# Moving the output gating of a head pair ahead of the next pair's scores in a fused LayerNorm, attention and int8 gate kernel

## The reference

```
xn = layernorm(x)                             # x: 4 x 4096 x 1024
q, k, v = split(xn @ qkv_weights)             # 16 heads of 64
a = softmax(causal(q @ k.T / 8))
s = a @ v
x_q = clip(round(xn / x_scale), -128, 127)    # x_scale = amax(|xn|) / 127, per row
g = silu((x_q @ weight_q.T) * x_scale * weight_scale + bias)
out = x + s * g
```

## Time and profile before

| | us |
|---|---|
| median of 3 runs | 1623.84 |
| lowest, highest | 1619.31, 1631.77 |
| the profiled execution's time | 1625.46 |
| its span, slowest core (core 4) | 1623.9 |
| spans of the eight cores | 1610.6 to 1623.9 |
| mean granted TensorE clock of the eight cores | 0.788 to 0.821 |

### The profile page before, as it was taken

How to read it: one execution, slowest core, us unless ns; L and a number is a source line. 1 busy time by engine, 2 the same in 40 slices (tenths; PEclk the granted TensorE clock), 3 DMA queues, 4 the chain that set the end, 5 groups by cost and what they waited for, 6 DMA issues and landing times.

```text
span 1623.9 us, 17793 instructions; the slowest of 8 cores (1610.6 to 1623.9 us)
## 1 busy us (share of the span) xinstructions
PE 1133.3 (70%) x5161; PEld 475.8 (29%) x5200; DVE 573.7 (35%) x1086; ACT 718.6 (44%) x905; POOL 301.3 (19%) x412
## 2 busy tenths in 40 slices
PE   0335545455565568887978887888688888888886
PEld 0112212212222225443333333333232333333332
DVE  0483472744735542137246227222621110110000
ACT  0121221212211123444354474466447787777776
POOL 1440421503324531013022012011200000000000
PEclk9867759567575666757977997888899998899998
DMA  7110000100002211011011011001000000000000
GB/s 114 52 40 0 26 27 0 39 14 26 26 13 65 64 47 40 26 52 53 7 46 46 7 52 40 7 21 40 20 7 20 14 14 14 14 21 11 9 14 20
DMA packets 24463, 47.46 MB, mean 29 GB/s; under 512 B 4272, under 2 KB 7472, under 8 KB 24368
## 3 DMA queue, kind: packets, MB, share of 16 engines
q1 hardware_dynamic: 15552, 25.34, 5.2%
q0 software_dynamic: 8816, 20.98, 5.2%
HBM read 40.54 MB, written 8.39 MB: 30 GB/s over the span
## 4 chain that ended last, share of the span: by engine, by line
PE 36%; DVE 23%; ACT 20%; issue 8%; POOL 5%; DMA 5%; DVEq 1%; ACTq 0%; POOLq 0%; SPq 0%
ACT eT L772 16%; PE Oa L789 5%; PE pm L551 4%; PE Ob L793 4%; PE pm L534 3%; DMA xst<-x 3%; DVE t_r L430 3%; PE sT L727 3%; DVE t_b L433 3%; PE pm L843 3%; PE pm L581 3%; PE pm L847 3%; DMA w8n<-w 2%; DVE t_g L428 2%; DVE bnst L240 2%
## 5 line engine op out<-in xcount | busy, mean ns | idle before, releaser
L772 ACT ACTIVATE eT<-sT 128x1024 bf16<-128x1024 f32 (+1 forms) x576 | 548.4, 952 | 331.1 <-PE sT L733 192.8
L789 PE MATMUL Oa<-eT,v_aug 128*65 128x512 bf16 (+1 forms) x576 | 245.3, 426 | 2.8 <-ACT eT L772 0.4
L793 PE MATMUL Ob<-eT,v_aug 128*65 128x512 bf16 (+1 forms) x576 | 233.2, 409 | 0.0
L727 PE MATMUL sT<-qT,kTa 64*128 64x512 bf16 x448 | 182.8, 417 | 63.0 <-ACT eT L772 61.5
L733 PE MATMUL sT<-qT,kTa 64*128 64x512 bf16 x448 | 185.7, 424 | 0.0
L892 POOL DMA_DIRECT2D out<-outs x32 | 24.4, 763 | 800.6 <-DVE outs L885 700.3
L828 DVE TENSOR_TENSOR wpr<-Oa,gT 64x512 bf16<-64x512 f32 x32 | 21.9, 683 | 370.0 <-PE Ob L793 369.2
L301 PE MATMUL sT<-Wqk,xnK 128*128 128x512 bf16 x244 | 106.5, 611 | 51.4 <-ACT xnK L289 40.3
L727 PEld LDWEIGHTS sT<-qT,kTa 64*128 64x128 bf16 x448 | 40.2, 94 | 267.0 <-issue 265.0
L789 PEld LDWEIGHTS Oa<-eT,v_aug 128*65 128x65 bf16 x576 | 68.7, 119 | 101.2 <-issue 88.8
L551 PE MATMUL pm<-Wv,xnq 128*128 128x512 bf16 x247 | 74.6, 452 | 27.9 <-DVE v_aug L558 21.8
(11 more groups left out here) (122 smaller groups left out, 1581.4 us busy)
## 6 DMA issues: line engine op xcount, KB each, us to landing
xst<-x SPq DMA_DIRECT2D x96, 256.0 KB, 2.9
xres<-xr POOLq DMA_DIRECT2D x32, 256.0 KB, 3.6
out<-outs POOLq DMA_DIRECT2D x32, 256.0 KB, 2.8
Wqk<-wq POOLq DMA_DIRECT2D x1, 1024.0 KB, 14.2
Wqk<-wk POOLq DMA_DIRECT2D x1, 1024.0 KB, 24.1
Wv<-wv POOLq DMA_DIRECT2D x1, 1024.0 KB, 30.4
w8n<-w POOLq DMA_DIRECT2D x4, 256.0 KB, 2.6
wscb<-wsc SPq DMA_DIRECT2D x4, 0.5 KB, 5.2
```

What stands on the lines that cost most here:

```text
L727: t.matmul(sT[par][:, o:o + w], kTa[0:64, P, 128 * jb:128 * jb + 128], qT[P][0:64, qb + o:qb + o + w], start=True, stop=True), waits=w0)
L772: s.activation(eT[pe3][:].rearrange("p (b n) -> p b n", b=2)[:, :, o:o + w], sT[par][:].rearrange("p (b n) -> p b n", b=2)[:, :, o:o + w], ...
L789: sc.emit("tensor", lambda t: t.matmul(Oa[:, o:o + w], v_aug[:, jb, 65 * hA:65 * hA + 65], eT[pe3][:, o:o + w], start=(jb == 0), stop=(jb ...
L793: c_av = sc.emit("tensor", lambda t: t.matmul(Ob[:, o:o + w], v_aug[:, jb, 65 * hB:65 * hB + 65], eT[pe3][:, 512 + o:512 + o + w], start=( ...
```

## The change

The part of the gating that is due at a unit is taken out at the head of the unit, ahead of `flush_av`, the scores and the exponential. For pairs of more than 4 units the list of units goes from 0, 2, 3, 4 to 0, 2, 4, 5. No instruction is added or removed.

```diff
-            pops_at = (0, 1, 2, 3) if njb <= 4 else (0, 2, 3, 4)
+            pops_at = (0, 1, 2, 3) if njb <= 4 else (0, 2, 4, 5)
             for jb in range(njb):
                 if P == 0 and jb == 4 * c - 1:
                     drain_pre()
-                do_pop = att["pend_gate"] and jb in pops_at
+                if att["pend_gate"] and jb in pops_at:
+                    close_open()
+                    att["pend_gate"].pop(0)()
                 if jb >= 3:
                     flush_av()
...
                 att["sT_rd"][par] = c_ex
-                if do_pop:
-                    close_open()
-                    att["pend_gate"].pop(0)()
```

## The result

| | before | changed |
|---|---|---|
| median of 10 runs, us | 1627.71 | 1581.82 |
| lowest to highest, us | 1619.31 to 1631.77 | 1574.94 to 1584.89 |
| span of the profiled execution, slowest core, us | 1623.9 | 1579.9 |
| mean granted clock of the eight cores | 0.788 to 0.821 | 0.791 to 0.820 |

The ratio is 0.972, with a 95% interval of 0.9699 to 0.9742: 2.8% faster. The forecast was 1581.5 us, the range 1557 to 1606.

What follows compares the result with a forecast made beforehand. No engine is full on average; waits at pair ends cost time, with ScalarE's exponentials setting the late stretch and TensorE chunks 1 to 4. Gains 26 + 13 + 3 + 2 = 44 us from 1625.5 give 1581.5 us, range 1557 to 1606.

Steps and rivals of the forecast that it cites:

- A: Start of the last AV at a pair end; times such as A + 1.9 are us after it.
- rows 3: Timeline of one late pair end before the change: two TensorE gaps, together 2.18 us; ga2 at A + 3.33.
- The ten late pair ends: Pair ends over 1232 to 1611.3 us, where ScalarE's exponentials set the time: 2.6 us each, 26 us in all.
- holds: Case at a late pair end: the clock stays full, 0.75 us of ScalarE's waits remain, gain 3.55 us.
- falls as before: Case at a late pair end: the clock falls as before, 2.6 of 4.3 us of waits remain, gain 1.7 us.
- The eleven and the seven: Eleven double-gap pair ends in chunks 1 to 4, 13 us; seven with projections or transposes in the first units, 2 us.
- of opposite sign: 0: Moving gb1 and gb2 behind their unit's pump: effects within 5 us and opposite, counted 0, range -5 to +5.
- Chunk 0: Three pair ends with all units on the diagonal; ga2 now behind s0, waiting some 0.5 us: 3 us in all.
- The sign of the clock: Sign in the profile after: mean granted clock above 0.79, with the stretches at 0.50 shorter.
- The clock holds everywhere: Rival: late ends give 35.5 us, the eleven 30 us, with 5 more 1555 us; chance 10%.
- The rival that ga2 starves ScalarE: Rival "slower": ga2 ahead of s2 delays exp2 by 1.6 us at the low clock; 22 us lost, 1647 us; chance 4%.
- Only the floor: Rival: the clock falls early and stays low; only the 1.07 us TensorE gap per end is won, 1600 us; chance 11%.

Runs made afterwards that it cites:

- the two single moves: Kernel before with only ga1 (copies of the row sums) moved to its unit's head: 1621.4 us, ratio 0.9989; with only ga2 moved: 1645.5 us, ratio 1.0137.
- by themselves: The changed order only at the ten late pair ends, the kernel before's order everywhere else: 1610.6 us, ratio 0.9893.
- the filling: Changed kernel plus four unread 504-column matmuls ahead of ga2 at pair ends of more than four units: 1567.6 us, ratio 0.963.

## Why the prediction was right

- **The mechanism.** The copies at A + 0.36, ga2 at A + 1.9, one gap of 1.1 us in place of 2.18: measured A + 0.37, A + 1.89 and 1.13. That both moves are needed was the forecast's reading of rows 3, and the two single moves (one changes nothing, the other is 1.4% slower) show it. The copy beside VectorE's read still takes 0.59 us.
- **The ten late pair ends: 26 forecast, 18.4 on core 4, 14.6 as a mean over the cores, 17 by themselves.** The step that was mis-sized is the clock. I took the middle between "holds" (3.55 us each) and "falls as before" (1.7 us each), reasoning that the quiet stretch gets 2 us shorter. It fell at all ten, only for less time at some of them. Both "falls as before" and the share of "holds" were too high. At the five pair ends of core 4 at which it fell for as long as before, the pair became 1.0 us shorter (0.7 to 1.1), which is the one gap of 1.07 us, the floor, and no more. At the five at which the fall was half as long, it became 2.7 us shorter (2.1 to 3.0). So the order itself is worth about 10 us at the late pair ends, and the rest is time at the higher clock. The size of the case in which it holds was nearly right: where the filling kept the clock up, 0.87 us of waits remained, against 0.75. I also misread rows 4 a little: of the 1.43 us that TensorE is busy before the fall, 1.03 are one-column matmuls, not half.
- **The eleven and the seven: 13 + 2 forecast, 25.4 on core 4, 23.8 as a mean.** The copies and ga2 account for 15.3 of it on core 4 and for 19.2 by the means. The rest is gb2, which I had put at 0 with 5 us either way; it won 5 to 10. The step "of opposite sign: 0" is the one that failed, and its reason too: the pump's transposes wait more for the outputs now, not less, and a part of what wins is a projection that no longer waits 2.1 to 2.6 us behind VectorE's outputs in the second pair of chunk 3, which the forecast did not look at.
- **Chunk 0: 3 forecast, 3.9 measured.** The three pairs took 10.8 to 11.0 us each instead of 12.0 to 12.4, 1.0 to 1.5 us less, against 1.0. (The rest of the 5.7 us in the table is the first pair of chunk 1, one of the seven.) The wait of ga2 at the first pair end went from 1.59 to 0.25 us, since it stands behind s0 and finds the copies nearly done:

```profile
612.65 0.55 PE L842 MATMUL pm<-idf_s,rows 1*128 1x1 f32 x2 [0.25 <-ACT rows L824]
```

- **The pair ends with projections in the first units** kept their wait for `pm`: ga2 waited 3.5 us in 4 places for the evacuation on ScalarE, against 3.0 us in 4 before. The forecast had them wait as long.
- **The sum.** By the means over the cores: late 11.4 too much, chunks 1 to 5 8.8 too little, chunk 0 with the first pair of chunk 1 1.3 too little. They cancel to within 2 us. On core 4 they are 7.6, 10.4 and 2.7, and 4.9 us that this execution spent more before anything had changed close the gap. That the point was hit within 1 us is luck; the direction and the interval are what the reasoning had earned.
- **The sign of the clock.** I had named a mean granted clock above 0.79 as a sign. It told nothing: core 4 had 0.794 before and has 0.791 now, and the mean over the cores went from 0.800 to 0.808.
- **The rivals.** "The clock holds everywhere" did not happen, and with it falls the rule of the Trainium skill that was weighed (TensorE: Matmul & The Clock Gate, HAM oscillation), that idle stretches between bursts throttle the clock, if it is read as the whole story: in the kernel with ga2 in four pieces TensorE was busy 12.94 of 13 us at the lower level. The rival that ga2 starves ScalarE is real, but only without the copies' move. "Only the floor" had the right price for the order itself at the late pair ends, and was wrong for chunks 1 to 5.

## What to carry to other kernels

When an engine has two waits in a row in front of a block, look whether they hang on one another through another engine: moving one instruction alone may win nothing or lose, and the pair wins. Ask of every small instruction on TensorE what it costs in time at the head of the queue; eight one-column fp32 matmuls took 1.8 to 3.4 us at each of 32 places of this kernel, and bf16 operands took nearly all of it away. A forecast that sums terms can hit the total with wrong terms, so compare it stretch by stretch, and on all cores: the slowest core of one execution had gained 18.4 us where the eight gained 14.6 on average.

## What the runs showed that I had not expected

- With one-column fp32 matmuls spread over the units the granted clock stays at 0.50 (1.2 GHz) for 6.8 to 13.7 us at a late pair end, in one of them with TensorE busy 99.5% of the time, and the kernel takes 80 us more, in part through waits for `pm`. With the eight kept together, in the changed kernel, it stays there for 3.4 or 6.8 us.
- A filled gap and a short block together leave the clock at 1.00 at all 80 late pair ends; either alone leaves 49 or 70 falls.
- Four matmuls of 504 columns whose results nobody reads make the kernel 14 us faster, by standing in a gap of 1.1 us.
- One-column matmuls follow each other at 0.025 us with bf16 operands and at 0.22 us with fp32 ones, nine times as long.
